# L2 and L3 experts of a four-layer decoder: rows that carry their token's number, answers scattered to token order, weight copies on ScalarE and VectorE

## The reference, cut to what matters

```python
# layer 2: 16 experts, best two, 320 places each
weights = top_vals / (top_vals.sum(-1, keepdims=True) + 1e-06)
slot = jnp.where(valid, flat_sel * capacity + ranks, sentinel)
padded = zeros.at[slot].set(jnp.repeat(xf, 2, axis=0)).reshape(E, capacity, d)
h = jax.nn.gelu(jnp.einsum('ecd,edf->ecf', padded, w1), approximate=False)
out_padded = jnp.einsum('ecf,efd->ecd', h, w2).reshape(sentinel, d)
gathered = jnp.where(valid[:, None], out_padded[slot], 0)
out = (gathered * weights.reshape(-1)[:, None]).reshape(T, 2, d).sum(axis=1)
# layer 3: 8 experts, best one, plus one shared expert
xs = x * sigmoid(top_logit)[:, None]
moe_out = ((silu(xs @ gate[e]) * (xs @ up[e])) @ down[e])   # e = the token's best expert
out = moe_out + silu(x @ shared_gate) * (x @ shared_up) @ shared_down
```

## Time and profile before

| | us |
|---|---|
| median of 3 runs (1881.9 to 1884.6) | 1884.1 |
| the profiled execution | 1888.33 |
| its span, first to last instruction | 1886.5 |
| mean granted TensorE clock | 0.899 of full |

### The profile page before, as it was taken

The page is one execution under the profiler, slowest core; times in us unless marked ns, Lnnn a source line. Parts: engine busy times, 40 slices in busy tenths (PEclk is TensorE's granted clock), DMA queues, the critical chain, the costliest instruction groups (busy, mean ns, idle before and its releaser), DMA issues. The chain is left out here.

```text
span 1886.5 us, 29434 instructions
## 1 busy us (share of the span) xinstructions
PE 1496.5 (79%) x10887; PEld 830.3 (44%) x10887; DVE 848.9 (45%) x2355; ACT 684.7 (36%) x1391; POOL 488.1 (26%) x573
## 2 busy tenths in 40 slices
PE   6898899995689999886997899770442489999683
PEld 4343434442544444464464344460332245555463
DVE  4555345542445556455114665263124545553332
ACT  2344414333147667552430334440112224334211
POOL 5533053310021110100004343003233524431055
PEclk9999899997999999896999999885786789999787
DMA  7000000000000000000004000000220000000022
GB/s 222 20 2 1 1 1 1 2 1 1 0 1 1 1 1 1 1 1 1 1 1 165 1 1 1 1 1 24 77 76 26 12 12 13 7 7 2 0 63 69
DMA packets 46432, 38.58 MB, mean 20 GB/s; under 512 B 4725, under 2 KB 40537, under 8 KB 46297
## 3 DMA queue, kind: packets, MB, share of 16 engines
q1 hardware_dynamic: 41408, 29.66, 5.2%
q0 software_dynamic: 3072, 6.30, 1.2%
q10 hardware_dynamic: 1816, 0.81, 0.2%
HBM read 25.81 MB, written 10.94 MB: 19 GB/s over the span
## 5 line engine op out<-in xcount | busy, mean ns | idle before, releaser
L1327 ACT ACTIVATE scores_L_experts_L<-L3x_psL 128x512 f32<-128x512 f32 x128 | 76.4, 597 | 173.4 <-PE L3x_psL L1190 169.8
L1364 DVE CUSTOM_DVE_ANT_0 L3x_junk<-L3x_psS,L3x_mask_rows 128x256 f32<-128x256 f32 x224 | 86.2, 422 | 92.6 <-PE L3x_psS L1152 84.5
L1190 PE MATMUL L3x_psL<-identb,L3x_mask_parts 128*128 128x256 bf16 x768 | 96.2, 276 | 0.0
L870 ACT ACTIVATE L0x_probs<-L0x_psL 128x512 f32<-128x512 f32 x96 | 52.1, 594 | 114.5 <-PE L0x_psL L683 79.3
L870 ACT ACTIVATE L2a_probs<-L2a_psL 128x512 f32<-128x512 f32 x96 | 52.1, 594 | 104.2 <-PE L2a_psL L681 69.4
L870 ACT ACTIVATE L0a_probs<-L0a_psL 128x512 f32<-128x512 f32 x96 | 52.1, 594 | 100.7 <-PE L0a_psL L681 65.0
L1172 PE MATMUL L3x_psL<-L3x_qm,ctx_T 32*128 32x512 f32 x256 | 73.5, 649 | 11.8 <-DVE L3x_mx L1364 11.3
L1190 PEld LDWEIGHTS L3x_psL<-identb,L3x_mask_parts 128*128 128x128 bf16 x768 | 70.4, 98 | 21.5 <-issue 13.7
L2878 POOL DMA_INDIRECT packed_rows<-h,slot x32 | 30.9, 966 | 143.6 <-POOLq L89 134.2
L1601 PE MATMUL L1a_psL<-L1a_soft_near,neg_tri 128*128 128x512 f32 x128 | 67.9, 612 | 0.2 <-DVE L1a_soft_near L1808 0.2
L1152 PE MATMUL L3x_psS<-L3x_km,L3x_qT 32*128 32x512 f32 x224 | 66.4, 670 | 1.9 <-DVE L3x_mx L1364 1.9
(11 more groups left out here) (792 smaller groups left out, 3937.1 us busy)
## 6 DMA issues: line engine op xcount, KB each, us to landing
packed_rows<-zeros SPq DMA_DIRECT2D x1, 2560.0 KB, 20.9
L2f_rows<-packed_rows SPq DMA_DIRECT2D x8, 320.0 KB, 3.5
unpacked_rows<-L2f_y SPq DMA_DIRECT2D x8, 320.0 KB, 2.7
experts_L_L<-in_L_ffn_w_dram SPq DMA_DIRECT2D x1, 2048.0 KB, 8.4
scores_L_experts_L<-in_L_ffn_w_dram SPq DMA_DIRECT2D x1, 2048.0 KB, 8.2
L3x_mask_rows<-in_mask_Bx1xSxS_ff_dram SPq DMA_DIRECT2D x8, 256.0 KB, 2.8
L3f_rows<-packed_rows SPq DMA_DIRECT2D x5, 256.0 KB, 4.7
unpacked_rows<-L3f_y SPq DMA_DIRECT2D x5, 256.0 KB
```

Source lines behind the costliest of these rows:

```text
L870: nc.scalar.activation(probs[:, half, a, k, :], psL[i % RING][:], ACT.Exp, scale=scale).then_inc(s_prob, 1)
L1190: last = nc.tensor.matmul(at[:, :, t * P:(t + 1) * P], parts[:, b % 2, i, t, u * P:(u + 1) * P], two, start=False, stop=i == PARTS - 1, sk ...
L1327: nc.scalar.activation(probs[:, half, a, k, :], psL[i % RING][:], ACT.Exp).then_inc(s_prob, 1)
L1364: last = nc.vector.tensor_tensor_reduce(out=junk[:, i, :], in0=psS[a][:, i * S:(i + 1) * S], in1=mrow[:, b % 2, t, :], scale=1.0, scalar=L ...
```

## The change

Rows grow from 128 to 130 numbers (`ROW2`, `ROW3`): column 128 is the number of the row in token order that the answer belongs to, column 129 in layer 2 the weight of this choice. Rows of the buffers that no token fills get numbers behind the answers (`blank`), so every row has a place. The answers of an expert pair (L2) or of a group of tiles (L3) are scattered by GpSimd straight to token order, after each pair or group; at the end SyncE loads them back with plain DMAs. In layer 2 VectorE keeps the two extra columns (`side`, `ids`), and the weight is applied as the answers leave PSUM. In layer 3 the weight copies go to ScalarE (gate and up, 512 columns) and VectorE (down, 256 columns), four buffers deep. The buffers of layer 3 are tensors of their own, and five DMAs clear and number the buffers in the first attention block.

```diff
+def blanks(w):
+    return [
+        (rows(w["packed"], SLOTS2, 0, D), zeros(SLOTS2)),
+        (rows(w["packed"], SLOTS2, D, ROW2), w["blank"][:, :, 0:2]),
+        (rows(w["unpacked"], 2 * B * S, 0, D), zeros(2 * B * S)),
+        (rows(w["sorted"], TILES3 * P, 0, D), zeros(TILES3 * P)),
+        (rows(w["sorted"], TILES3 * P, D, ROW3), w["blank"][:, 0:TILES3, 2:4]),
+    ]
...
 # slots_of_two
+                for c in range(4):
+                    at = slice(c * NT // 4, (c + 1) * NT // 4)
+                    nc.scalar.copy(rows[:, 1, at, 0:D], rows[:, 0, at, 0:D])
...
+                for i in range(2):
+                    steps.step(nc.vector.tensor_copy(rows[:, i, :, D], w["token"][:, i, :]))
...
-                    steps.step(nc.vector.scalar_tensor_tensor(home[:, i, :], at[:, :, 0], float(E * capacity), fits[:, :, 0],
-                                                              ALU.add, ALU.mult))
...
 # slot_experts, GpSimd
-                for i in range(2):
-                    pool.wait_ge(s_store[i], 16 * (PAIRS // 2))
-                for t in range(NT):
-                    for i in range(2):
-                        nc.gpsimd.indirect_dma_start(back_rows[:, t, i, :], None, unpacked,
-                                                     bass.IndirectOffsetOnAxis(ap=home[:, i, t:t + 1], axis=0)).then_inc(s_back[t // TPB], 16)
+                for c in range(PAIRS):
+                    pool.wait_ge(s_y, c + 1)
+                    for t in range(TILES):
+                        nc.gpsimd.indirect_dma_start(unpacked, bass.IndirectOffsetOnAxis(ap=ids[:, c, t:t + 1], axis=0),
+                                                     y[:, c % 2, t, :], None).then_inc(s_store[c % 2], 16)
...
 # slot_experts, SyncE
+                for i in range(2):
+                    sp.wait_ge(s_store[i], 16 * TILES * (PAIRS // 2))
+                for b in range(B):
+                    for i in range(2):
+                        first = i * B * S + b * S
+                        sp.dma_start(back_rows[:, i, b * TPB:(b + 1) * TPB, :],
+                                     unpacked[first:first + S, :].rearrange("(t p) d -> p t d", p=P)).then_inc(s_back[b], 16)
...
 # slot_experts, VectorE
+                    nc.vector.tensor_copy(ids[:, c, :], xe[:, c % 3, :, D])
+                    nc.vector.tensor_copy(side[:, c, :, :], xe[:, c % 3, :, D:ROW2]).then_inc(s_side, 1)
...
+                        last = nc.vector.tensor_scalar(y[:, c % 2, t, :], made, side[:, c, t, 1:2], None, ALU.mult)
...
-                            last = nc.vector.scalar_tensor_tensor(mem.x[:, t, :], back_rows[:, t, i, :], weight[:, i, t:t + 1], mem.x[:, t, :],
-                                                                  ALU.mult, ALU.add)
+                        nc.vector.tensor_tensor(mem.x[:, at, :], mem.x[:, at, :], back_rows[:, i, at, :], ALU.add).then_inc(s_x, 1)
...
 # one_expert, GpSimd
-                for i in range(TILES):
-                    at = pool.value_load(offset[0:1, i:i + 1], min_val=0, max_val=(E - 1) * ONE)
-                    if i >= RING:
-                        pool.wait_ge(s_tdown, i - RING + 1)
-                    nc.gpsimd.tensor_copy(mine[:, i % RING, :], every[:, bass.ds(at, ONE)]).then_inc(s_mine, 1)
+                for i in range(TILES):
+                    if i % CHUNK == 0:
+                        pool.wait_ge(s_ids, i // CHUNK + 1)
+                        pool.wait_ge(s_y, i // CHUNK + 1)
+                    nc.gpsimd.indirect_dma_start(unpacked, bass.IndirectOffsetOnAxis(ap=ids[:, i:i + 1], axis=0),
+                                                 y[:, i, :], None).then_inc(s_store, 16)
...
 # one_expert, SyncE
+                sp.wait_ge(s_store, 16 * TILES)
+                for c in range(CHUNKS):
+                    sp.dma_start(back_rows[:, c * CHUNK:(c + 1) * CHUNK, :],
+                                 unpacked[c * WIDE:(c + 1) * WIDE, :].rearrange("(t p) d -> p t d", p=P)).then_inc(backs[c], 16)
...
 # one_expert, ScalarE; VectorE has own_down, alike with s_tdown, [DOWN:ONE] and s_down_mine
+                def own_up(i):
+                    at = act.value_load(offset[0:1, i:i + 1], min_val=0, max_val=(E - 1) * ONE)
+                    if i >= RING:
+                        act.wait_ge(s_tup, i - RING + 1)
+                    nc.scalar.copy(mine[:, i % RING, 0:DOWN], every[:, bass.ds(at, DOWN)]).then_inc(s_mine, 1)
...
+                act.wait_ge(s_offset, 1)
+                for i in range(RING - 1):
+                    own_up(i)
...
+                        if i + RING - 1 < TILES:
+                            own_up(i + RING - 1)
...
 # one_expert, VectorE
+                dve.wait_ge(s_offset, 1)
+                for i in range(RING - 1):
+                    own_down(i)
                 keep_rows(0)
                 for i in range(TILES):
                     if i % CHUNK == 0 and i // CHUNK + 1 < GROUPS:
                         keep_rows(i // CHUNK + 1)
                     tile_hidden(i)
+                    if i + RING - 1 < TILES:
+                        own_down(i + RING - 1)
```

More of the change, by code:

```diff
@@ L433, in first_experts, with rows, zeros @@
     ]
+def blanks(w):
+    def rows(buffer, n, a, b):
+        return buffer[0:n, a:b].rearrange("(a p) d -> p a d", p=P)
+    def zeros(n):
+        return w["zeros"][:].unsqueeze(1).to_broadcast([P, n // P, D])
+    return [
[5 more added lines that the diff above has]
+    ]
 def last_experts(w, dram):
@@ L460, in quad_heads @@
 def quad_heads(nc, mem, w, name, *, wq, wk, wv, wo, wq_rot=None, wk_rot=None, bq=None, bk=None, bv=None, bo=None,
-               cross=False, mask, scale, loads=(), clear=None):
+               cross=False, mask, scale, loads=(), clear=()):
     KINDS = ((0, 0), (1, 0), (1, 1))
@@ L2772, in first_best, with slots_of_two @@
     steps.step(nc.vector.tensor_tensor(onehot, desc, key.to_broadcast(wide), ALU.is_equal))
-def slots_of_two(nc, mem, w, name, logits, weight, slot, home, E, capacity):
+def slots_of_two(nc, mem, w, name, logits, rows, slot, E, capacity):
     with ExitStack() as ctx:
@@ L2838, in _, with slot_experts @@
                     steps.step(nc.vector.tensor_scalar(slot[:, i, :], at[:, :, 0], float(E * capacity), None, ALU.add))
-def slot_experts(nc, mem, w, name, h_all, weight, slot, home, w1, w2, packed, unpacked, E, capacity):
+def slot_experts(nc, mem, w, name, rows, slot, w1, w2, packed, unpacked, E, capacity):
     PAIRS, CHUNKS = E // 2, w1.shape[2] // P
@@ L3226, in shared_add, with own_down @@
                                             ALU.add).then_inc(s_add, 1)
+                def own_down(i):
+                    at = dve.value_load(offset[0:1, i:i + 1], min_val=0, max_val=(E - 1) * ONE)
+                    if i >= RING:
+                        dve.wait_ge(s_tdown, i - RING + 1)
+                    nc.vector.tensor_copy(mine[:, i % RING, DOWN:ONE], every[:, bass.ds(at + DOWN, ONE - DOWN)]).then_inc(s_down_mine, 1)
                 def keep_rows(j):
                     dve.wait_ge(s_turned, j + 1)
+                    at = slice(group(j)[0], group(j)[-1] + 1)
+                    nc.vector.tensor_copy(ids[:, at], xe[:, at, D]).then_inc(s_ids, 1)
                     if j >= 2:
```

105 lines of the change are left out of this document (54 added, 51 removed).

## The result

| | median us | runs from to | ratio to before (95%) |
|---|---|---|---|
| before | 1883.0 | 1880.0 to 1884.6 | |
| changed | 1858.2 | 1857.3 to 1858.7 | 0.9867 (0.9853 to 0.9881) |

The forecast was 1858. One thing must be said at once, because the number can't be understood without it: on two other chips the same changed kernel gained nothing (1884.5 and 1884.8), and on a third it gained 1.25% again (1858.2). The profiled execution of the changed kernel took 1858.1 us, its span is 1856.2 us.

What follows compares the result with a forecast made beforehand. Two serial tails of GpSimd gathers were taken as the bound; moving them beside the experts saves 15.6 us in L2 and 10.7 in L3, so 1884.1 - 26.3 = 1858 us, range 1850 to 1869.

Steps and rivals of the forecast that it cites:

- the hole of 7 us: Before L3's tiles, ScalarE and VectorE stand still from 1808.7 to 1816.0; its absence would save up to 5 us more.
- the sum: Whole kernel: savings in the L2 and L3 tails total -26.3 us, giving 1858; 63% chance.
- 15.6: L2 experts and tail: scatters beside the experts replace the gathers, ending at 1425.1 against 1440.75, -15.6 us.
- 10.7: L3 experts and tail: scatters replace gathers and copies leave GpSimd, ending at 1875.8 against 1886.5, -10.7 us.
- the rival with the split rows: Filling scatters in L2 and L3: 520-byte rows cut in two, up to 0.96 us more each, 1904; 4%, middle case 3%.
- the one with scatters 0.2 us slower beside work: L2 and L3 scatters: 0.2 us slower each over the 47 that count, +9 us, 1867; 7%.
- Three weight copies ahead of `keep_rows(0)`, +1.4: Start of L3's tiles: three VectorE down-weight copies at 0.66 us delay the turned rows TensorE waits for, +1.4 us.
- The last seven scatters begin as the y copy ends, with no earlier backlog: End of L3: seven scatters run behind the group before the last's y, GpSimd done 8.5 us later, no backlog.
- The loop up to there takes as long as before: L3 until the group before the last has y: unchanged from 1854.93 except 1.6 us of added costs.
- The loop itself, the part I was least sure of: L3 tile loop: copies on ScalarE and VectorE fit within TensorE's 1.46 us a tile, so zero cost.
- GpSimd becomes the bound of the stage, not TensorE: L2 experts: five scatters a pair take GpSimd 6.3 us against TensorE's 5.3; forty take 50.6 us.
- My 3% for "no change": Whole kernel: 0.03 chance that the time stays the same, change being told from none at about 3.8 us.

Runs made afterwards that it cites:

- copies alone: Kernel before with only layer 3's weight copies moved from GpSimd to ScalarE and VectorE, ring of four; 1891.5 us, ratio 1.0025.
- e8: Whole changed kernel, unedited, timed again against the kernel before on another chip, with late updates; 1884.8 us, ratio 0.9996.
- e5: Whole changed kernel, unedited, timed again against the kernel before on another chip, with late updates; 1884.5 us, ratio 0.9992.
- e1: Kernel before, unchanged, profiled a second time to see whether the 7 us stall comes back; span 1883.2 us, chip median 1884.8.

## Why the prediction was right, and where it was not

**How much is luck.** The forecast was 1858, and 1853 if the hole of 7 us should be missing; it was missing, and the time was 1858.2. That the two numbers agree so closely is luck by about 3 us. So the hole's 3.7 us (below) made good what the rest of the sum had promised too much. Against the second trace of the kernel before the changed one is 27.0 us shorter, 23.3 without the hole, where the sum had 26.3: L2f gives 14.3 us for 15.6, L3f without the hole 9.6 for 10.7, and what lies ahead of L2f and between L2f and L3f is 0.7 us longer. Side by side on the chip without late updates the gain is 23.1; its interval (18 to 29) holds the sum too. The mechanism was right where updates come in time: both tails of gathers are gone, GpSimd's scatters bound L2, and L3's loop keeps its pace.

**L2, right to 0.5 us, step by step.** First scatter 1356.47 (forecast 1356.2), last end 1406.7 (1406.5), SyncE 1408.0 (1407.8), first addition 1410.8 (1411.3), 1.72 us a batch entry, end 1424.7 (1425.1). The gain of the stage, from its first rows to the next stage, is 15.3 us in the two first traces, and 14.3 against the second trace of the kernel before, whose tail of gathers was shorter. A row of 520 bytes costs what one of 512 costs (0.96), so the rival with the split rows is out, and so is the one with scatters 0.2 us slower beside work.

**L3, the sum right, its terms not.** From the first instruction of L3f to the end the traces differ by 13.5 us where I had 10.7. 3.7 of them are the hole: rows had landed by about 1818.0 in the kernel before, and TensorE turned them at 1821.64. I left that out of the sum and put it in the range, as I could not name what held the engines. Without it 9.8 are left for my 10.7. Three terms are off:
- *Three weight copies ahead of `keep_rows(0)`, +1.4*: nothing. VectorE was done with them at 1801.2, before the first rows were turned; with the hole gone the wait for the rows' DMA covers them. Where the shared expert ends late they cost 1.9 directly and 2.9 through the slower first tiles (copies alone).
- *The last seven scatters begin as the y copy ends, with no earlier backlog*: they begin 1.0 us later (1836.38 after 1835.39). 0.74 of that is what GpSimd takes to be released, as behind the group before (1831.33 after 1830.59), and 0.25 a backlog, as the last full group came 4.8 us after the one before and not 5.8.
- *The loop up to there takes as long as before*: TensorE ran the first tiles largely at the lower of its two clocks, 1.2 GHz: mean granted clock 0.61 between 1803.3 and 1807.0, after it had waited 2.6 us for the rows; the kernel before has 1.00 from 1824 on. From the first turn to the end of the last y copy but one that makes 34.4 us for 33.3. The loads and additions at the end take 6.3 us and not 5.6.

The loop itself, the part I was least sure of, was rightly costed at zero: 26.4 us between first and last y copy for 27.0, with ScalarE busy 23.6 of 35 us. Register loads take 0.28 us there and their second instruction 0.15, as GpSimd's did.

**What the forecast missed.** Its sum was made for TensorE's results being seen at once, and on four of the five chips of the experiments they are not while scatters run. The step that fails there is "GpSimd becomes the bound of the stage, not TensorE", and in L3 the zero for the loop: L2f is 10.3 us longer (99.2 for 88.9) and L3f 16.0 (107.7 for 91.7), together the whole gain of 26. Of the 16.0, 9.5 are the tile loop (35.9 for 26.4), so that the moved scatters cost about 20; 6.2 (in e8) lie ahead of the first turned rows, where the hole of the kernel before is back and the three weight copies stand on the path behind it. It is a rival that I did not have: not slower scatters, but scatters that slow their neighbours. The trace of before showed its sign, two engines idle beside 16 scatters with no releaser that fits (the rows name a DMA of layer 2, long over), and I priced only its vanishing, not its spreading, though the change puts 63 more scatters beside TensorE's work. My 3% for "no change" was far too low for a forecast that should hold on any chip; that it held rests on the chip on which the change was timed.

A caution on the 24.8 us between the medians. Three of the four runs behind the median of before are those shown with its profile, whose trace has held updates; the fourth, made beside the changed kernel, took 1880.0. Where both kernels ran side by side on a chip without them, the gain was 23.1 (1881.3 to 1858.2).

## What to carry to other kernels

Work that moves from a serial tail to a place beside other work is to be priced twice: for the engine that does it, and for what its neighbours lose; an idle time whose releaser does not fit, found in the trace of before, is a price tag for that, not noise. Measure a change that adds scatters beside matmuls on more than one chip before you believe its gain. Hand over small pieces: releasing answers sooner cut the time from the last answer to the end of its scatter by 3 us, and on a chip with held updates it kept 8 us that the coarser version lost.

## What the runs showed of the hardware

- On four of the five chips TensorE's semaphore updates come up to 8 us late while GpSimd issues indirect DMAs 1.26 us apart. Behind a burst they arrive in a bunch, in L2's experts mostly 0.8 to 1.1 us after the last scatter has landed, in L3's tile loop as it lands (1837.02 to 1837.18 in e5, with the landing recorded at 1837.15); some arrive within a burst. None of 1,756 updates outside such stretches is late in any trace, and none in the same stretch when the scatters are 2.55 us apart. VectorE's updates in L2's experts are on time (none late of 21 recorded in e5); ScalarE's record has gaps there, so that it is left open. The Trainium skill, "Perfetto Trace Analysis", section "Tensor Engine Instruction (MATMUL, LD_WEIGHTS)", says that this engine's update is sent when PSUM has acknowledged all bytes, and that the end of a matmul is an estimate of the profiler. So the delay can lie in that acknowledgement or in the update's way; for TensorE no run here tells which.
- It is not TensorE alone. At the end of the 32 gathers of the kernel before, VectorE waits for its own updates. In e1 two additions end at 1436.80, their semaphore rises at 1438.02, and the next addition starts at 1438.05:

```profile
1438.05 0.61 DVE L2988 SCALAR_TENSOR_TENSOR x_resid<-L2f_back_rows,weight,x_resid 128x128 f32<-128x128 f32 x2 [1.25 <-DVE x_resid L2988]
```

- A VectorE copy from SBUF to SBUF of 0.41 us, repeated without pause, makes a scatter 0.12 us longer. The Trainium skill, "SBUF — State Buffer", section "SBUF: two separate sides", says that GpSimd can't write descriptors during such a copy; the measured price is small, and the measurement decides.
- A scatter of 128 rows takes 0.96 us of GpSimd and 1.26 us of its queue for rows of 512 and of 520 bytes alike, and 2.55 us if each waits for the landing of the one before.
